# Two conditional residual layers: all four single LoRA products ahead of the mask products, and the opening transfers dealt out anew between two queues

## The reference

```python
masked_w = L0_cond_weight * L0_cond_mask[None]          # (8, 256, 256)
w_bot = einsum('bg,got->bot', cond_8, masked_w)
x = x + einsum('bnt,bot->bno', x, w_bot) + L0_cond_bias
out = einsum('btc,oc->bto', x, L1_cond_W_base) + L1_cond_b_base
lora = einsum('bter,eor,be->bto', einsum('btc,erc->bter', x, As), Bs, cond_8)
x = x + out + lora * 2.0
```

## Time and profile before

| | |
|---|---|
| timed runs | 56.59, 57.09, 57.01 us, median 57.01 |
| profiled execution | 56.67 us, span 54.9 us |
| busy, share of span | PE 50.9 us (93%), DVE 39.4 (72%), ACT 31.7 (58%), POOL 31.7 (58%) |
| transfers | 11.79 MB, mean 215 GB/s |
| PE instructions | 330 |

### The profile page before, as it was taken

The page is one execution under the profiler, slowest core; times in us unless marked ns, Lnnn a source line. Parts: engine busy times, 40 slices in busy tenths (PEclk is TensorE's granted clock), DMA queues, the critical chain, the costliest instruction groups (busy, mean ns, idle before and its releaser), DMA issues.

```text
span 54.9 us, 973 instructions
## 1 busy us (share of the span) xinstructions
PE 50.9 (93%) x330; PEld 45.6 (83%) x330; DVE 39.4 (72%) x64; ACT 31.7 (58%) x53; POOL 31.7 (58%) x30
## 2 busy tenths in 40 slices
PE   2998999999999999999999999999999999999900
PEld 2988889999998978998898889889889889888800
DVE  0049799939599996999999987689939809805030
ACT  1939950434719499629606992992992940850800
POOL 4001727099920099999994999999999910000000
PEclk9999999999999999999999999999999999999999
DMA  0699999999999997000720072063063054059582
GB/s 0 128 366 261 332 373 408 418 415 416 406 412 403 403 418 317 36 0 0 288 100 0 0 294 100 0 254 134 0 236 146 0 220 163 0 200 370 194 287 96
DMA packets 5476, 11.79 MB, mean 215 GB/s; under 512 B 608, under 2 KB 1376, under 8 KB 5472
## 3 DMA queue, kind: packets, MB, share of 16 engines
q1 hardware_dynamic: 5184, 11.35, 55.9%
q10 hardware_dynamic: 288, 0.39, 2.0%
HBM read 7.54 MB, written 4.19 MB: 214 GB/s over the span
## 4 chain that ended last, share of the span: by engine, by line
PE 87%; DMA 5%; ACT 1%; DVE 1%; issue 1%
PE ps_out L532 14%; PE ps_out L462 13%; PE ps_out L466 13%; PE ps_out L470 13%; PE ps_merge L462 7%; PE ps_merge L466 7%; PE ps_merge L470 7%; DMA lora_sb<-factors_B_dram 5%; PE ps_lora L476 3%; PE ps_lora L466 3%; PE ps_lora L462 3%; PE ps_lora L470 3%; ACT B_hi L232 1%; DVE out_sb L453 1%; PE ps_out L596 1%
## 5 line engine op out<-in xcount | busy, mean ns | idle before, releaser
L191 POOL TENSOR_TENSOR W_lo<-W,W_hi 128x512 fp32r<-128x512 f32 x8 | 13.2, 1652 | 2.2 <-ACT W_hi L240 2.2
L358 DVE TENSOR_TENSOR x_lo<-x_sb,x_hi 128x1024 fp32r<-128x1024 f32 x8 | 11.9, 1486 | 0.2 <-ACT x_hi L260 0.2
L462 PE MATMUL ps_out<-x_hi,M_hi 128*128 128x512 f32 (+1 forms) x32 | 9.8, 388 | 0.0
L466 PE MATMUL ps_out<-x_lo,M_hi 128*128 128x512 f32 (+1 forms) x32 | 9.7, 384 | 0.0
L470 PE MATMUL ps_out<-x_hi,M_lo 128*128 128x512 f32 (+1 forms) x32 | 9.7, 383 | 0.0
L253 ACT ACTIVATE M_hi<-ps_merge 128x512 fp32r<-128x512 f32 x8 | 4.8, 595 | 7.5 <-PE ps_merge L470 7.5
L197 POOL TENSOR_TENSOR W_lo<-W,W_hi 128x512 fp32r<-128x512 f32 x6 | 8.8, 1458 | 0.1
L201 POOL TENSOR_TENSOR W<-W,ident 128x256 f32<-128x256 f32 x6 | 6.5, 1093 | 3.7 <-DVE x_lo L358 3.7
L260 ACT ACTIVATE x_hi<-x_sb 128x1024 fp32r<-128x1024 f32 x8 | 8.4, 1056 | 0.0
L532 PE MATMUL ps_out<-packs_sb 128*128 128x128 f32 x64 | 8.2, 278 | 0.0
L373 DVE TENSOR_SCALAR out_sb<-ps_out,bias_sb 128x512 f32<-128x512 f32 x7 | 5.2, 746 | 4.1 <-PE ps_out L470 4.0
(11 more groups left out here) (58 smaller groups left out, 71.6 us busy)
## 6 DMA issues: line engine op xcount, KB each, us to landing
x_sb<-xT_dram SPq DMA_DIRECT2D x8, 512.0 KB, 10.8
outT_dram<-out_sb SPq DMA_DIRECT2D x15, 256.0 KB, 2.3
packs_sb<-packs_dram SPq DMA_DIRECT2D x7, 288.0 KB, 5.9
rows_sb<-rows_dram SPq DMA_DIRECT2D x1, 384.0 KB, 7.2
base_sb<-base_dram ACTq DMA_DIRECT2D x1, 256.0 KB, 3.9
outT_dram<-out_sb SPq DMA_DIRECT2D x2, 128.0 KB, 1.8
packs_sb<-head_dram SPq DMA_DIRECT2D x1, 192.0 KB, 3.8
packs_sb<-rest_dram SPq DMA_DIRECT2D x1, 160.0 KB, 4.9
```

The lines of the kernel that those rows point to most:

```text
L191: pool.tensor_tensor(W1_lo[:, b % W1BUF], W1[:, b % W1BUF], W1_hi[:, b % W1BUF].bitcast(f32), ALU.subtract).then_inc(w1lo_done, 1)
L358: nc.vector.tensor_tensor(x_lo[:, b % XBUF], x_sb[:, b], x_hi[:, b % XBUF].bitcast(f32), ALU.subtract).then_inc(xlo_done, 1)
L462: nc.tensor.matmul(out, hi_l, hi_r, start=(n == 0), stop=False)
L466: nc.tensor.matmul(out, hi_l, lo_r, start=False, stop=False)
```

## The change

TensorE: LoRA 2 and 3 move up behind LoRA 0 and 1 and write to `ps_merge`, which is free then, so they no longer wait for W1; in `lora_first` the first product of LoRA 1 goes ahead of those with A_lo; the eight packs' mask products follow in one piece; the first merge halves get a wait for W1(2) and W1(3), which are read from the same PSUM. There are 27 warm-up products for 28. VectorE makes W1(1), (2) and (3) earlier among the W0 steps. ScalarE and GpSimd do W1_hi(2) and W1_lo(1), (2) ahead of the first identity of W0, and W1_hi(3), W1_lo(3) earlier too. Transfers: SyncE issues factors_B (now with the condition), factors_A, head, and then the packs. ScalarE issues rest and base, after a wait for the identity (`ident_done`), and it no longer waits for factors_A ahead of B_hi.

```diff
@@ -32,10 +32,10 @@
     SINGLE = 4
     XBUF = 4
     W1BUF = 4
-    WARM = 28
+    WARM = 27
     assert packs.shape == (NQ - 1, P, PACKW)
 
-    OB0, OB1, OA, OBT = NB, NB + NT, NB + 2 * NT, NB + 2 * NT + C
+    OBT, OB0, OB1, OA = NB, NB + C, NB + C + NT, NB + C + 2 * NT
     cut = MIXW + C
 
     with ExitStack() as ctx:
@@ -58,7 +58,7 @@
             return (packs_sb[:, at:at + EXPW].rearrange("p (k c) -> p k c", k=KQ),
                     packs_sb[:, at + EXPW:at + PACKW].rearrange("p (j t) -> p j t", j=NT))
 
-        lora_sb = sb("lora_sb", [P, OBT + C])
+        lora_sb = sb("lora_sb", [P, OA + C])
         cond_er = lora_sb[:, 0:NB]
         bias0 = lora_sb[:, OB0:OB0 + NT]
         bias1 = lora_sb[:, OB1:OB1 + NT]
@@ -105,6 +105,8 @@
         ps_merge = [pb(f"ps_merge{i}", [P, NT, C]) for i in range(2)]
         ps_lora = [pb(f"ps_lora{i}", [P, NT, C]) for i in range(2)]
         ps_mix = ps_out
+
+        ps_first = ps_lora + ps_merge
         ps_last = ps_lora[0][:, 0, :]
 
 
@@ -143,9 +145,9 @@
 
         @block.sync
         def _(sp):
-            sp.dma_start(lora_sb[:, 0:OBT], factors_A).then_inc(lora_arrived, 16)
+            sp.dma_start(lora_sb[:, 0:OB0], factors_B).then_inc(B_arrived, 16)
+            sp.dma_start(lora_sb[:, OB0:OA + C], factors_A).then_inc(lora_arrived, 16)
             sp.dma_start(packs_sb[:, 0:cut], head).then_inc(mix_in, 16)
-            sp.dma_start(packs_sb[:, cut:MIXW + PACKW], rest).then_inc(pack_in[0], 16)
             for q in range(1, NQ):
                 at = MIXW + q * PACKW
                 sp.dma_start(packs_sb[:, at:at + PACKW], packs[q - 1]).then_inc(pack_in[q], 16)
@@ -202,14 +204,15 @@
                                    ALU.add).then_inc(eye_done, 1)
 
             w1_lo(0)
+            w1_lo(1)
+            w1_lo(2)
             pool.wait_ge(w0_done, NQ // 2)
             pool.tensor_tensor(W0[:, 0:2, 0, 0:H], W0[:, 0:2, 0, 0:H], ident[:, :].unsqueeze(1).to_broadcast([P, 2, P]),
                                ALU.add).then_inc(eye_first, 1)
-            w1_lo(1)
             pool.wait_ge(ramp_hi, 1)
             pool.tensor_tensor(W0_lo[:, :, :, 0:H], W0[:, 0:2, :, 0:H], W0_hi[:, :, :, 0:H].bitcast(f32),
                                ALU.subtract).then_inc(ramp_first, 1)
-            w1_lo(2)
+            w1_lo(3)
 
             pool.wait_ge(w0_done, NQ)
             pool.wait_ge(xlo_done, 1)
@@ -217,7 +220,6 @@
             eye(3)
             w0_lo(2)
             eye(4)
-            w1_lo(3)
             w0_lo(3)
             for b in range(4, NB):
                 if b + 1 < NB:
@@ -269,22 +271,24 @@
                 nc.scalar.activation(out_sb[:, b % 2, 0, :], ps_out[b % 2 * NT][:, :], ACT.Identity,
                                      bias=bias_sb[:, 0, b:b + 1]).then_inc(out_done[0], 1)
 
-            act.dma_start(lora_sb[:, OBT:OBT + C], factors_B).then_inc(B_arrived, 16)
 
             act.wait_ge(warm_set, 1)
             nc.scalar.activation(table_sb[:, :], warm[:, 0:1], ACT.Copy)
+
+            act.wait_ge(ident_done, 1)
+            act.dma_start(packs_sb[:, cut:MIXW + PACKW], rest).then_inc(pack_in[0], 16)
             act.dma_start(base_sb[:, :, :], base.rearrange("p (j o) -> p j o", j=NT)).then_inc(base_in, 16)
 
             act.wait_ge(B_arrived, 16)
-            act.wait_ge(lora_arrived, 16)
             for b in range(NB):
                 b_hi(b)
             w1_hi(0)
             w1_hi(1)
+            w1_hi(2)
 
             act.wait_ge(eye_first, 1)
             nc.scalar.activation(W0_hi[:, 0:2, :, 0:H], W0[:, 0:2, :, 0:H], ACT.Copy).then_inc(ramp_hi, 1)
-            w1_hi(2)
+            w1_hi(3)
             split_x_hi(0)
 
             act.wait_ge(rows_in, 16)
@@ -293,7 +297,6 @@
             for b in range(2):
                 act.wait_ge(eye_second, 1)
                 nc.scalar.activation(W0_hi[:, b, :, H:C], W0[:, b, :, H:C], ACT.Copy).then_inc(ramp_hi, 1)
-            w1_hi(3)
             m_hi(0)
             split_x_hi(1)
             w0_hi(2)
@@ -327,7 +330,7 @@
 
             def w1(b):
                 dve.wait_ge(lora_mm, b + 1)
-                nc.vector.tensor_tensor(W1[:, b], ps_lora[b % 2][:, :, :], base_sb[:, :, :],
+                nc.vector.tensor_tensor(W1[:, b], ps_first[b][:, :, :], base_sb[:, :, :],
                                         ALU.add).then_inc(w1_done, 1)
 
             def w1_pair(b):
@@ -391,21 +394,20 @@
             dve.wait_ge(B_arrived, 16)
             for b in range(4):
                 b_lo(b)
-
             dve.wait_ge(base_done, NT)
             w1(0)
             b_lo(4)
             b_lo(5)
+            w1(1)
             w0(0)
+            w1(2)
             w0(1)
-            w1(1)
             w0(2)
             w0(3)
+            w1(3)
             w0(4)
-            w1(2)
             w0(5)
             w0(6)
-            w1(3)
             w0(7)
             dve.wait_ge(w0_done, NQ)
             nc.vector.tensor_tensor(W0[:, 0:2, 1, H:C], W0[:, 0:2, 1, H:C], ident[:, :].unsqueeze(1).to_broadcast([P, 2, P]),
@@ -479,10 +481,10 @@
                 pe.wait_ge(ahi_done, 1)
                 pe.wait_ge(bhi_done, 1)
                 term(0, 0, A_hi, B_hi, first=True)
+                pe.wait_ge(bhi_done, 2)
+                term(1, 0, A_hi, B_hi, first=True)
                 pe.wait_ge(alo_done, 1)
                 term(0, 0, A_lo, B_hi)
-                pe.wait_ge(bhi_done, 2)
-                term(1, 0, A_hi, B_hi, first=True)
                 term(1, 0, A_lo, B_hi)
                 pe.wait_ge(blo_done, 1)
                 term(0, 0, A_hi, B_lo, last=True)
@@ -498,10 +500,9 @@
             def lora(b):
 
                 pe.wait_ge(blo_done, b + 1)
-                pe.wait_ge(w1_done, b - 1)
                 for j in range(NT):
                     cols = slice(j * P, (j + 1) * P)
-                    mm = product(ps_lora[b % 2][:, j, :],
+                    mm = product(ps_first[b][:, j, :],
                                  [(A_hi[:, cols], A_lo[:, cols], B_hi[:, b], B_lo[:, b])])
                 mm.then_inc(lora_mm, 1)
 
@@ -572,17 +573,15 @@
             for _ in range(WARM):
                 nc.tensor.matmul(ps_merge[0][:, 0, 0:P], warm[:, :], warm[:, :], start=True, stop=True)
             lora_first()
-            for q in range(4):
+            lora(2)
+            lora(3)
+            for q in range(NQ):
                 mixed(q)
-            lora(2)
-            mixed(4)
-            mixed(5)
-            lora(3)
-            mixed(6)
-            mixed(7)
             for b in range(2):
                 pe.wait_ge(ramp_hi, 1)
                 pe.wait_ge(w1lo_done, b + 1)
+
+                pe.wait_ge(w1_done, b + 3)
                 merge_half(b, 0, (ramp_first, 1))
             lora_pair(4)
             for b in range(2):
@@ -636,8 +635,8 @@
     masks = mask.reshape(NT, P, NQ, TQ).transpose(1, 2, 0, 3).reshape(P, NQ, NT * TQ)
     packs = np.concatenate([mix.reshape(P, P), np.concatenate([experts, masks], axis=2).reshape(P, -1)], axis=1)
     A_er = As.reshape(G * R, C)
-    lora = np.concatenate([np.repeat(cond.T, R, axis=0), halves(bias0[:, None]), halves(bias1[:, None]),
-                           A_er, Bs.transpose(0, 2, 1).reshape(G * R, C)], axis=1)
+    lora = np.concatenate([np.repeat(cond.T, R, axis=0), Bs.transpose(0, 2, 1).reshape(G * R, C),
+                           halves(bias0[:, None]), halves(bias1[:, None]), A_er], axis=1)
 
     rows = np.concatenate([halves(base), np.broadcast_to(bias0, (P, C))], axis=1)
     xT = np.ascontiguousarray(x.transpose(0, 2, 1).reshape(NB, NT, P, TOK).transpose(0, 2, 1, 3).reshape(NB, P, NT * TOK))
@@ -645,7 +644,7 @@
     first = P + packs.shape[1] // NQ - P // NQ
     arrays = {"head": packs[:, :cut], "rest": packs[:, cut:first],
               "packs": packs[:, first:].reshape(P, NQ - 1, -1).transpose(1, 0, 2), 
-              "factors_A": lora[:, :-C], "factors_B": lora[:, -C:], "base": halves(base.T), "rows": rows, "xT": xT}
+              "factors_A": lora[:, NB + C:], "factors_B": lora[:, :NB + C], "base": halves(base.T), "rows": rows, "xT": xT}
     arrays = {n: np.ascontiguousarray(a) for n, a in arrays.items()}
 
     nc = bacc.Bacc("TRN2", target_bir_lowering=False, num_devices=1)
```

## The result

The changed kernel takes 57.48 us (median of four, 57.22 to 57.62); the kernel before takes 56.80 (median of four, 56.30 to 57.09). The executions of a kernel differ by 1% and more, so ratios here are taken from the fast executions of both alone, and that of this change is 1.0163, with an interval of 1.0097 to 1.0229: slower by 1.0 to 2.3%. I had forecast 56.5 and a small gain. The time lies just inside my range; the direction was wrong. The profiled execution has 57.62 us and a span of 55.8, against 56.67 and 54.9 before.

A forecast was written before the change was run, and what follows sets the result against it. TensorE, 87% of the chain's span, bounds the kernel, so the end moves with the marker: adds 6.12 + 0.91 + 8.13 = 15.16 against 15.51, gain 0.35; 56.84 - 0.35 = 56.5 us, range 55.9 to 57.5.

The forecast's parts named there:

- TensorE's own order: TensorE's LoRA and mask products alone would put the marker at 14.81, gain 0.70; as rival deciding the time: 56.1, chance 0.25.
- mask products that wait for W0: Sign of a wrong forecast: TensorE's mask products waiting on the four banks; packs were forecast ready before W0(3) at T+4.4.
- The chain from T: From T, VectorE's start of W1(0), forecast at 7.03, through GpSimd's W1_lo, identity and W0_lo to the marker at T + 8.13.
- marker: Start of TensorE's W0_lo terms (line 470) in the first merge halves, 15.51 before, forecast 15.16; the end moves with it.
- The start of the adds: GpSimd starts adding the identity to the base matrix, 5.28 before; forecast 6.12, bounds 5.6 and 6.6.
- the sum in bytes: Base's landing from 891 to 1153 kB at earlier rates, 4.85 to 5.86, middle 5.36; GpSimd's adds start 0.76 behind.
- the packs' share: Bytes of the second pack on the other queue moved ahead of base's end: between none and as much as base, 262 kB.
- the 6.47 from which I had said the change loses: Start of GpSimd's base adds from which late base decides and the change loses: 15.51 - 8.13 - 0.91.
- the base matrix comes late: Rival: base lands late among packs; adds at 7.1 lose 0.63, at 7.3 0.83, time 57.5 to 57.7; chance 0.21.
- Behind the marker: Second merge halves: W0_hi and W0_lo for the other columns done by 17.0, over 0.5 us ahead of use; no cost.
- The clock rival: A new 0.35 us TensorE stall drops the products behind it to 1.2 GHz for 2 us, losing 1 us (57.5); chance 0.03.
- the 0.35 or 0.70: Gains at the marker: 0.35 net with TensorE waiting for W0_lo; 0.70 if the adds start before 5.77.

The follow-up runs named there:

- e5: Changed kernel with rest and base swapped on ScalarE's queue (base first, rest second), both still behind the wait for the identity; median 56.48 us, no ratio.
- e9: Changed kernel with the condition's 8 columns (4 KB) issued first on ScalarE's queue, at once, ahead of the wait for the identity; ratio to before 1.0166.
- e10: Changed kernel with rest on SyncE's queue behind head, base alone behind the identity, and the 4 KB condition issued at once on ScalarE's queue; ratio to before 0.9980.
- e14: Changed kernel with ScalarE issuing rest and base only once B is in, instead of after the wait for the identity; one run, 60.15 us.
- e16: Changed kernel without ScalarE's wait for the identity ahead of rest and base, the same kernel as e15, timed; ratio to before 1.0070.
- e1: Changed kernel's order of work on all engines, with the transfers dealt out as in the kernel before; ratio to before 0.9990.
- e13: Changed kernel with all opening transfers on SyncE's queue (B, A, head, base, rest, packs) and none on ScalarE's; ratio to before 0.9967.
- e15: Changed kernel without ScalarE's wait for the identity ahead of rest and base; one run, 56.36 us.
- e8: Changed kernel with only B_lo 4 and 5 moved on VectorE, ahead of its wait for the base matrix; median 57.82 us, no ratio.
- e12: Changed kernel with W0(0) to W0(3) right behind W1(0), W1(1), W1_lo(2) later, B_lo 4 and 5 before base, rest on SyncE; ratio to before 1.0057.
- e7: Changed kernel without the wait for the identity: ScalarE issues rest at once and base behind the activation; median 58.31 us, no ratio.
- e3: Changed kernel with base issued at once on ScalarE's queue, without the wait for the identity, and rest behind it; median 58.66 us, no ratio.
- e17: Changed kernel without the wait for the identity and with rest on SyncE's queue behind head, base alone on ScalarE's; ratio to before 1.0116.
- e6: Changed kernel with rest on SyncE's queue behind head, ScalarE issuing base alone behind the wait for the identity; median 56.61 us, no ratio.
- e2: Kernel before, with its old order of work, given the changed kernel's transfers; ratio to before 1.0228.
- e4: Changed kernel with W0(0) to W0(3) right behind W1(0), W1(1); W1(2), W1(3), B_lo 4 and 5 later, W1_lo(2) behind the first W0_lo; ratio to before 1.0301.

## Why the prediction was wrong

*TensorE's own order: right up to the mask products, and a little better.* First LoRA product at 4.05 forecast, 3.81 measured, since A was in at 3.37 and B at 2.94. LoRA end 7.35 forecast, 7.06 measured. No waits for rest or packs: right. A miss: mask products that wait for W0 were one of my signs of being wrong, and they came, since W0 started late. The mask products ended at 14.98 and not at 14.25, no earlier than before (14.95). It had no effect only because W0_lo, ready at 16.3, was later still.

*The chain from T: right.* W1_lo(1) to the identity without a pause on GpSimd, at T + 5.28 (5.30 forecast), marker at T + 8.11 (8.13). In after, e5, e9, e10, e14 and e16, the kernels of this order in which TensorE waited for GpSimd at the marker, the distance is 8.09 to 8.12. The adds took 0.90 from their start to T (0.91), undisturbed. 

*The start of the adds: this step failed.* I put it at 6.12 with bounds of 5.6 and 6.6, and it was 7.34. The step was the sum in bytes: so many bytes ahead of base's end, at the rates of the earlier trace rows, plus 0.76. Two of its terms were wrong.

The rates were those of the kernel before; the engines now moved 196 GB/s from 3 to 4 us instead of 366. That is the smaller part. The changed kernel had moved my 891 kB by 5.2 us and my 1153 kB by 5.95; with these times the same sum gives 6.3, which is 0.2 of the 1.2 us.

The larger part, about 1 us, is what went ahead of base's end. I had bounded the packs' share at 262 kB, as much as base. By 7.0 us SyncE's queue (q1) had moved 1.09 MB, of which B, A and head are 0.47, so 0.62 MB of packs were ahead. And nearly all of base was in long before: of the 288 packets of rest and base on ScalarE's queue (q10) 271 were under way by 5.5 us, and the last 17, with 0.02 MB, were spread over 1.5 us, beside 0.49 MB of packs. The queues of the changed kernel (packets, MB, share of the engines), first up to 5.5 us, then from 5.5 to 7:

```profile
q10 hardware_dynamic: 271, 0.40, 24.3%
```

```profile
q1 hardware_dynamic: 240, 0.49, 97.7%
q10 hardware_dynamic: 17, 0.02, 4.2%
```

In the kernel before all 288 were under way by 4.75 us. So base's landing was set by a few late packets among the packs, which no sum of bytes gives; 0.76 was measured on a transfer with a shorter tail.

Put into the rest of the sum, 7.34 gives 7.34 + 0.91 + 8.13 = 16.38; measured 16.35. So this start made the whole miss: 1.2 us there, against a slack of 0.35 between the forecast of that start and the 6.47 from which I had said the change loses.

The rival that came true is "the base matrix comes late"; 0.21 was too little for it, and its own price for adds at 7.3, a marker 0.83 later, fits the 0.84. That the time still lies in my range is owed to its wide upper end, 57.5. I had its condition and not its weight: a new wait and a second transfer ahead of base are both on the path, and no row of before bounded their effect.

*Behind the marker: right, but near.* Nothing was late in the changed kernel up to apply 0, and the merge halves' new wait for W1 cost nothing. But VectorE's identity for the second columns took 1.49, beside GpSimd's W1_lo(3), where it took 0.42 before; I had not reckoned with that. The clock rival did not come: the granted clock of the profiled execution is 0.998.

*What remained of the gain.* e1 shows that also with base in time the order would have brought 0.22, and not the 0.35 or 0.70: TensorE's own order then ends at 15.29 instead of 14.81, since the LoRA products are done at 7.68. e13, with the products at 3.81 and the base adds at 5.00, has 15.10, a gain of 0.41, and the shortest span, 54.5. Its interval, 0.9921 to 1.0013, holds both the forecast gain (0.35 us would be 0.994) and none. No version was shown faster than the kernel before.

What stays open is why the DMA engines slow down near 3 us, and why base's last packets come so late. In e15 286 of the 288 were under way by 4.75 us and base still landed at 5.9, in e16 266 by 5.5 us; with the transfers of the changed kernel base landed at 7.2 to 7.4 in four traces and at 8.1 in the fifth (e8).

## What to carry over

When a change gives a matrix a new place among the first transfers, treat its landing as unknown: a landing is that of its last packet, and neither the rates of the old order nor a bound on the bytes beside it carry over. The range has to take in the later issue and 1 to 2 us more (from issue to landing 3.9 became 5.3, and 6.1 in e8). If one transfer must come first, put it ahead of the others on the same queue, as e13 did (base in at 4.8). Find the one start time from which two chains part and put the chance on that; here the rest of the sum was right to 0.03 us. And before shortening a chain, look at what is queued behind it on the same engine within the next 8 us: in e12 a marker 0.75 earlier brought nothing.

## What the runs showed of the hardware

- With a transfer of 160 or 256 KB issued at 0.73 or 0.97 on a second queue, A, issued at 1.17 on the first, was in at 4.5 to 4.8 instead of 3.3 (e7, e3, e17). e9 had it at 4.6 without one, so the large transfer is not the only way to a late A. The Trainium skill ("DMA: Bandwidth & Descriptors", section "Issuing engines are not separate DMA queues") says that all queues share the same engines and that a second one saves only issue time. The runs agree in that one queue (e13) was no slower than two; which bytes came first depended on the queues all the same: two kernels that had moved 0.84 MB by 5.0 us had base in at 4.8 (e13) and at 7.2 (after).
- A first moment of half pace. LoRA products come 0.20 to 0.21 apart until 4.8 in the changed kernel, 5.4 in e13, 6.1 in e6, at least 6.5 in e2, 8.8 in e3 and e7 and 9.1 in e17, and 0.12 after that, while the granted clock in the windows from 3 to 7 us is 1.00 in all of them. TensorE was idle just before the first product for 1.40 us in e3, 0.84 in e7 and 0.88 in e17, but also for 0.90 in e9, where the change of pace came at 6.0. The runs don't tell what sets it; it costs 0.09 us for each product. In e13 it is why the LoRA products end at 7.48 and not at 7.06.
- VectorE's B_lo takes 0.42 to 0.48 alone, 1.52 (e12) and 1.19 on average (two in e4) beside GpSimd's W1_lo. The Trainium skill ("SBUF — State Buffer", "Who interferes with whom") has the second read port of VectorE shared with GpSimd and locked by one at a time; the longer B_lo agree, and GpSimd's W1_lo pay less for it: two took 2.74 in e12 and 2.90 in e4, where the first two of each, beside VectorE's W1 and W0 steps, took 2.51.
